# Leaving the context sums of an attention unnormalised, with beta as moving columns, split latent keys and wide softmax steps

## The chip, the cores and the metric

One core of a Trainium2 chip runs the kernel. The metric is device time in microseconds; the kernel before takes 1115.04 us, the median of three runs (1113.75 to 1117.1).

## What is computed

x is 8 batches of 100 tokens with 512 features. Three residual steps follow each other, each on a layernorm of x: a gated linear recurrence, a cross attention and a routed feed-forward. The change touches the attention:

```python
xn = _layernorm(x, gamma_media, beta_media)      # x here: the context, 8 x 722 x 512
ln = _layernorm(latents, gamma_lat, beta_lat)    # latents: layernorm of x, 8 x 100 x 512
q = ln @ Wq + bq
kv = jnp.concatenate([xn, ln], axis=1) @ Wkv + bkv
k, v = jnp.split(kv, 2, axis=-1)                 # 8 heads of 128
sim = jnp.einsum('bhid,bhjd->bhij', q * DH ** (-0.5), k)
out = jnp.einsum('bhij,bhjd->bhid', jax.nn.softmax(sim, axis=-1), v)
return out_transposed @ Wo + bo
```

## The kernel before

Everything is in float32, but the large products run in a faster form: each operand is split in a high and a low part and `split_products` (L575) issues three matmuls, high by high, high by low and low by high. Most have 400 moving columns.

Keys and values are never formed. The **q projection** (`project` on PE, 100 to 190 us) makes q per head for four batches at a time (a "half") and multiplies it by Wk, which gives queries in the space of the context rows ("qt"). ACT and DVE take each product out of its bank into one of the `st` buffers (L2039 on DVE), and SyncE stores them to `scr_q`. The latents serve as keys as well: `latent_keys` on DVE (L2012, L2014) adds their two parts up and subtracts the media's beta into `lks`, of which there are two, SyncE stores them to `scr_keys`, later loads one batch (`lk`), and `keys_of_latents` splits it again.

The **attention loop** goes over 16 units u, two per batch b (g = 0, 1), a unit being 4 heads by 100 latents, 400 columns. The 822 rows are 7 chunks: 6 of 128 and one of 54. A step does the scores of unit u (80 matmuls; ACT copies each bank to `pa` with the rms scale of the rows, L1426) and then the context sums of unit u-1, in four column blocks dc (80 matmuls). In between are small products: `turn_maxima` (L1111) transposes the running maxima so that DVE can reduce them, `spread_maxima` (L1118) brings the shift back to all rows, `spread_sums` (L1123) adds the sums of weights over the rows by a matrix of ones. DVE takes maxima (L1862, L1870), finds the shift (L1880 to L1886, result `dg`), adds it (L1894), adds up the weights (L1902, L1906), forms the low part of the weights (L1914, L1679), takes the reciprocal of the sums (L1923, 128x400, `inv`) and multiplies each context block by it on the way out of the bank (L1933, `zf`); ACT then adds beta (L1449), since the rows carry gamma but no beta. ACT does the exponentials (L1435) and the high part of the weights (L1441). In between, DVE prepares the next batch: statistics of rows (L1661, L1668), whose means go to DRAM and come back along the free axis as `mrow` (L676, L681), centred rows (L1675), centred keys (L1823, L1832), queries and the low rows `xn_l`. The order on each engine is written out by hand; DVE, ACT and SyncE take their instructions in that order.

`zf` goes to `scr_z`. The **value products** come after the loop: for each of 2 halves and 8 heads a unit of z (128x1600, `zr`) is loaded, split (ACT `z_h` L1471, DVE `z_l` L1679), multiplied by Wv on PE (12 matmuls), and its result split again (ACT `ot_h` L1485, DVE `ot_l` L1955) for the product with Wo. A list of events, run through by PE, ACT and DVE alike, each doing its part, sets the order: V a value product and its split, U the split of a unit of z, Y the output product of 128 tokens. It begins

```python
tail = [("V", 0), ("C", 0), ("U", 4), ("V", 1), ("U", 5), ("V", 2), ("U", 6), ("V", 3), ("V", 4), ("U", 7),
        ("V", 5), ("U", 8), ("V", 6), ("U", 9), ("V", 7), ("U", 10),
```

## Time and profile before

| | |
|---|---|
| median of 3 runs | 1115.04 us (1113.75 to 1117.1) |
| profiled execution, its time | 1109.71 us |
| its span | 1108.0 us |
| busy: TensorE / VectorE / ScalarE / GpSimd | 1021.8 / 879.2 / 595.3 / 129.9 us |
| mean granted TensorE clock | 0.964 |
| DMA | 177.62 MB, mean 160 GB/s |

PE is TensorE's matmul side, DVE VectorE, ACT ScalarE, SP SyncE. A share of busy time is a mean over stages; what bounds a stage is read from its own waits. Times in a timeline count from the start of the span. A matmul's row gives its whole duration; those of one stream overlap, so their cost is the distance of two starts.

### The profile page before, as it was taken

Reading aid. Unit: us, or ns where it says so; the run is one execution under the profiler, and the core shown is the slowest. Engines: PE = TensorE matmul, PEld = TensorE weight load, DVE = VectorE, ACT = ScalarE, POOL = GpSimd, SP = SyncE. Lnnn points to the kernel's source line nnn. Section 1 sums busy time; section 2 is a strip of 40 time slices with the busy share of each in tenths; the row PEclk is TensorE's granted clock in tenths of the full one; section 3 lists DMA queues with packets and bytes.
Section 4 is the critical chain, followed back from the end, with each engine's and each line's share of the span. In section 5 each row is a group of like instructions: output and inputs, shape, how many; then the busy total and the mean of one; then the engine's idle time right before and its main releaser. Section 6 shows DMA issues by size and latency. Waiting matters only on the chain. (4 is left out here: it accounts for less than half of the span.)

```text
span 1108.0 us, 14839 instructions
## 1 busy us (share of the span) xinstructions
PE 1021.8 (92%) x5178; PEld 926.5 (84%) x5179; DVE 879.2 (79%) x1206; ACT 595.3 (54%) x790; POOL 129.9 (12%) x107
## 2 busy tenths in 40 slices
PE   8998989569999998998989989799998999999997
PEld 7978878569899898998989989688886888888886
DVE  6988644878989989899998986687576993965992
ACT  4525455424665536555365554457344783856881
POOL 3525400000000000000000000000012021211221
PEclk9999889779999999999999999989998999999999
DMA  9313969303151332513234110726935992984980
GB/s 283 104 66 117 278 184 299 97 30 121 44 187 62 107 121 68 177 58 126 91 111 150 44 49 12 270 109 235 308 121 144 331 371 79 343 288 147 363 295 21
DMA packets 105886, 177.62 MB, mean 160 GB/s; under 512 B 28049, under 2 KB 48017, under 8 KB 105827
## 3 DMA queue, kind: packets, MB, share of 16 engines
q1 hardware_dynamic: 104146, 172.30, 47.1%
q0 software_dynamic: 1680, 4.54, 1.2%
q8 instruction: 36, 0.59, 0.3%
q14 instruction: 24, 0.19, 0.0%
HBM read 142.19 MB, written 35.61 MB: 160 GB/s over the span
## 5 line engine op out<-in xcount | busy, mean ns | idle before, releaser
L579 PE MATMUL bank<-ph,xn_h 128*128 128x400 f32 x384 | 145.7, 380 | 25.1 <-issue 13.5
L1679 DVE TENSOR_TENSOR wsl<-stage,wsh 128x2048 fp32r<-128x2048 f32 x63 | 143.8, 2292 | 21.9 <-ACT wsh L1476 17.3
L580 PE MATMUL bank<-pl,xn_h 128*128 128x400 f32 x384 | 137.6, 358 | 0.0
L579 PE MATMUL bank<-qt_h,xt_h 128*128 128x400 f32 x384 | 137.4, 358 | 0.0
L581 PE MATMUL bank<-ph,xn_l 128*128 128x400 f32 x384 | 136.9, 357 | 0.0
L580 PE MATMUL bank<-qt_l,xt_h 128*128 128x400 f32 x384 | 132.8, 346 | 0.0
L581 PE MATMUL bank<-qt_h,xt_l 128*128 128x400 f32 x384 | 132.1, 344 | 0.0
L1476 ACT CAST wsh<-stage 128x2048 fp32r<-128x2048 f32 x63 | 120.5, 1920 | 11.5 <-PE bank L581 8.4
L1426 ACT ACTIVATE pa<-bank,rsr 128x400 f32<-128x400 f32 x96 | 56.9, 595 | 110.8 <-PE bank L581 107.3
L579 PEld LDWEIGHTS bank<-ph,xn_h 128*128 128x128 f32 x384 | 76.1, 198 | 33.0 <-issue 19.1
L1449 ACT ACTIVATE zf<-zf,gbm 128x400 f32<-128x400 f32 x64 | 39.8, 621 | 79.6 <-DVE zf L1933 79.6
L580 PEld LDWEIGHTS bank<-pl,xn_h 128*128 128x128 f32 x384 | 76.2, 198 | 2.6 <-issue 0.3
L581 PEld LDWEIGHTS bank<-ph,xn_l 128*128 128x128 f32 x384 | 76.1, 198 | 0.0
L579 PEld LDWEIGHTS bank<-qt_h,xt_h 128*128 128x128 f32 x384 | 72.7, 189 | 2.3
L580 PEld LDWEIGHTS bank<-qt_l,xt_h 128*128 128x128 f32 x384 | 72.6, 189 | 2.2
L581 PEld LDWEIGHTS bank<-qt_h,xt_l 128*128 128x128 f32 x384 | 72.5, 189 | 0.0
L579 PE MATMUL bank<-wsh,xg_h 128*128 128x512 f32 x160 | 64.3, 402 | 2.0 <-issue 2.0
L579 PE MATMUL bank<-wsh,ht_h 128*128 128x512 f32 x160 | 65.0, 406 | 0.0
L580 PE MATMUL bank<-wsl,xg_h 128*128 128x512 f32 x160 | 62.9, 393 | 0.0
L581 PE MATMUL bank<-wsh,xg_l 128*128 128x512 f32 x160 | 62.9, 393 | 0.0
L581 PE MATMUL bank<-wsh,ht_l 128*128 128x512 f32 x160 | 62.6, 391 | 0.0
L580 PE MATMUL bank<-wsl,ht_h 128*128 128x512 f32 x160 | 62.3, 390 | 0.0
(269 smaller groups left out, 2414.1 us busy)
## 6 DMA issues: line engine op xcount, KB each, us to landing
stage<-in_W SPq DMA_DIRECT2D x63, 1024.0 KB, 6.6
scr_q<-st SPq DMA_DIRECT2D x16, 800.0 KB, 6.5
qf<-scr_q SPq DMA_DIRECT2D x16, 800.0 KB, 5.2
scr_z<-zf SPq DMA_DIRECT2D x16, 800.0 KB, 3.5
zr<-scr_z SPq DMA_DIRECT2D x16, 800.0 KB, 6.0
rt<-in_ctxT SPq DMA_DIRECT2D x7, 1444.0 KB, 6.3
raw<-in_ctx SPq DMA_DIRECT2D x8, 768.0 KB, 4.9
raw<-in_ctx SPq DMA_DIRECT2D x8, 512.0 KB
```

What stands on the lines that cost most here:

```text
L579: pe.matmul(dest, lh, rh, start=start and k == 0, stop=False)
L580: pe.matmul(dest, lh, rl, start=False, stop=False)
L581: last = pe.matmul(dest, ll, rh, start=False, stop=stop and k == n - 1)
L1426: act.activation(pa[k][:, c, :], score_bank(u, c)[:, 0:GR], ACT.Identity, scale=rss[b % 2][:, c:c + 1]).then_inc(s_ev, 1)
L1449: act.activation(at, at, ACT.Identity, bias=gbm[:, 1, dc:dc + 1]).then_inc(s_zbeta, 1)
L1476: act.copy(wsh[q][:], (first_last if made_in_place else stage[q % 4])[:]).then_inc(s_wh, 1)
L1679: return dve.tensor_tensor(dst, src, high.bitcast(F32), ALU.subtract)
```

## The change

- **Context sums.** ACT copies each context block out of its bank unscaled (`context_out`, in place of `add_shift`); `weighted` on DVE is gone. `spread_sums` gives the sums with the latents on the partitions (four matmuls with one moving column), and the reciprocal is of 100x4. The inverses of a batch are stored to `scr_inverse` (`store_inverse`) and loaded as rows over all partitions (`load_inverse`, 128x400, three buffers `ivt`), one per value product. DVE multiplies the value product by its row (`normalised`), ACT's `ot_h` and DVE's `ot_l` (event "v") then read `ivt`.
- **Beta.** It isn't added to z any more; two extra moving columns hold it (high and low part), so that a value product gives beta times Wv as two columns, which DVE adds to bv (`cb`, first half only). In the first half of the q projection two columns do the same for the latents. POOL's `shift_latents` is gone.
- **Latent keys.** The tokens' two parts are stored as they are and loaded from there straight into the split keys; `latent_keys` and `keys_of_latents` are gone. The load waits for the scores of the batch before.
- **Wide steps.** Maxima in operations of 800, 800, 400 and 54x400, sums likewise, low and high weights as 1200, 1200 and 54x400. The rms scale moves from the weights to the rows (`rows_high`, `rows_low`: six pieces with a scale).
- **Order.** In the loop the maxima of unit u are turned after context block 0 and spread after block 1. `rows_stats` of batch b+2 moves to the end of the odd unit, the queries ahead of the shift of the even one; SyncE stores the means ahead of z. In the last unit `values_low(2)` moves ahead of the shift and `values_low(3)` behind.

```diff
+XB = 2
+ZB = 2
+NIV = 3
...
-    d_lt = dram("scr_keys", (B, P, ND, LK))
+    d_lt = dram("scr_keys", (2, P, ND, NTOK))
+    d_iv = dram("scr_inverse", (2, HEADS, HT))
...
-    tail = [("V", 0), ("C", 0), ("U", 4), ("V", 1), ("U", 5), ("V", 2), ("U", 6), ("V", 3), ("V", 4), ("U", 7),
-            ("V", 5), ("U", 8), ("V", 6), ("U", 9), ("V", 7), ("U", 10),
+    tail = [("V", 0), ("C", 0), ("U", 4), ("V", 1), ("v", 0), ("U", 5), ("V", 2), ("v", 1), ("U", 6), ("V", 3), ("v", 2),
+            ("V", 4), ("v", 3), ("U", 7), ("V", 5), ("v", 4), ("U", 8), ("V", 6), ("v", 5), ("U", 9), ("V", 7), ("v", 6),
+            ("U", 10), ("v", 7),
             ("Y", 0), ("A", 0), ("B", 0), ("Y", 1), ("A", 1), ("B", 1), ("T", 0), ("Y", 2), ("A", 2), ("L", 0),
-            ("B", 2), ("T", 1), ("V", 8), ("U", 11), ("L", 1), ("T", 2), ("V", 9), ("U", 12), ("V", 10), ("U", 13), ("L", 2),
-            ("V", 11), ("U", 14), ("V", 12), ("U", 15), ("V", 13), ("V", 14), ("V", 15),
+            ("B", 2), ("T", 1), ("V", 8), ("U", 11), ("v", 8), ("L", 1), ("T", 2), ("V", 9), ("U", 12), ("v", 9),
+            ("V", 10), ("U", 13), ("v", 10), ("L", 2), ("V", 11), ("U", 14), ("v", 11), ("V", 12), ("U", 15), ("v", 12),
+            ("V", 13), ("V", 14), ("v", 13), ("V", 15), ("v", 14), ("v", 15),
...
+                sp.dma_start(xt_h[:, :, MEDIA:KLOW + KLAST].bitcast(F32), d_lt[0][:, :, at:at + T]).then_inc(s_ltin, 16)
+                sp.dma_start(xt_h[:, :, KLOW + DUP:KLOW + DUP + KLAST].bitcast(F32), d_lt[1][:, :, at + LAT0:at + T]
+                             ).then_inc(s_ltin, 16)
+                sp.dma_start(xt_l[:, :, MEDIA:KLOW].bitcast(F32), d_lt[1][:, :, at:at + LAT0]).then_inc(s_ltin, 16)
...
+            def store_inverse(b):
+                sp.wait_ge(s_inv, 2 * b + 2)
+                if b:
+                    sp.wait_ge(s_ivd, 16 * b)
+                sp.dma_start(d_iv[b // HALF, :, b % HALF * T:(b % HALF + 1) * T].rearrange("h t -> t h"), iv[0:T, b, :],
+                             allow_slow_non_contiguous=True).then_inc(s_ivd, 16)
+            def load_inverse(k):
+                half, h = divmod(k, HEADS)
+                if k >= NIV:
+                    sp.wait_ge(s_otl, ot_done(k - NIV))
+                if half and not h:
+                    sp.wait_ge(s_ivd, 16 * B)
+                if k >= 2:
+                    sp.wait_ge(s_ivl[k % 2], 16 * (k // 2))
+                sp.dma_start(ivt[k % NIV][:], bc(d_iv[half, h], HT)).then_inc(s_ivl[k % 2], 16)
...
+                sp.wait_ge(s_s, KC * (2 * b + 2))
+                load_latent_keys(b + 1)
+                sp.wait_ge(s_ktl, keys_done(b + 1))
                 if b + 2 < B:
                     load_keys(b + 2)
-                    load_latent_keys(b + 2)
+                    store_mean(b + 2)
+                    sp.wait_ge(s_nr, (b + 1) * 2)
+                    load_mean(b + 2)
...
+                    wide, out_tokens = bank[u % 4][:, 0:extra + HT], bank[u % 4][:, extra:extra + HT]
+                    for c in range(ND):
+                        high, low = wq_h[:, c, h * P:(h + 1) * P], wq_l[:, c, h * P:(h + 1) * P]
+                        pe.matmul(wide, high, xa_h[:, c, tokens_and_shift], start=c == 0, stop=False)
+                        pe.matmul(out_tokens, high, xa_l[:, c, cols], start=False, stop=False)
+                        last = pe.matmul(wide, low, xa_h[:, c, tokens_and_shift], start=False, stop=c == ND - 1)
+                    last.then_inc(s_qp, 1)
...
                 pe.wait_ge(s_dg, u + 1)
-                pe.matmul(mbank[:, 0:GR], ones[:], sm[:], start=True, stop=True).then_inc(s_spread, 1)
+                for j in range(GH):
+                    last = pe.matmul(mbank[0:T, j:j + 1], sm[:, 0, j * T:(j + 1) * T], ones[:, 0:1], start=True, stop=True)
+                last.then_inc(s_spread, 1)
...
-                            pe.wait_ge(s_otl, ot_done(k - 4))
-                        split_products(
-                            pe, bank[k % 4][:, 0:HT].rearrange("p (b t) -> p b t", b=HALF),
-                            [((wv_h[:, c, h * P:(h + 1) * P], wv_l[:, c, h * P:(h + 1) * P]),
-                              (z_h[zh_of[k]][:, :, c, :], z_l[zr_of[k]][:, :, c, :])) for c in range(ND)], True, True
-                            ).then_inc(s_vp, 1)
+                            pe.wait_ge(s_on, k - 3)
+                        wide, narrow = bank[k % 4][:, 0:HT + ZB], bank[k % 4][:, 0:HT].rearrange("p (b t) -> p b t", b=HALF)
+                        for c in range(ND):
+                            high, low = wv_h[:, c, h * P:(h + 1) * P], wv_l[:, c, h * P:(h + 1) * P]
+                            pe.matmul(wide, high, z_h[zh_of[k]][:, c, :], start=c == 0, stop=False)
+                            pe.matmul(narrow, high, z_l[zr_of[k]][:, :, c, :], start=False, stop=False)
+                            last = pe.matmul(wide, low, z_h[zh_of[k]][:, c, :], start=False, stop=c == ND - 1)
+                        last.then_inc(s_vp, 1)
...
-                    if u == 1 and c == 0:
+                    if u == 1 and c == 1:
                         turn_maxima(0)
-                    elif u == 1 and c == 2:
+                    elif u == 1 and c == 3:
                         spread_maxima(0)
                     elif u > 1 and c == 3:
                         spread_sums(u - 1)
                 if u == 1:
-                    context(0, 0)
                     spread_sums(0)
-                    context(0, 1)
-                    turn_maxima(1)
-                    context(0, 2)
-                    spread_maxima(1)
-                    context(0, 3)
+                if u < NU - 1:
+                    context(u - 1, 0)
+                    turn_maxima(u)
+                    context(u - 1, 1)
+                    spread_maxima(u)
...
+            def weights_high(u, part):
+                k, cs = u % 2, slice(PARTS[part][0], PARTS[part][-1] + 1)
+                act.wait_ge(s_exp, NP * u + part + 1)
+                if MC not in PARTS[part]:
+                    act.copy(ph[k][:, cs, :], pa[k][:, cs, :]).then_inc(s_ph, 1)
                 else:
-                    act.copy(ph[k][0:DUP, c, :], pa[k][0:DUP, c, :])
-                    act.copy(ph[k][DUP:P, c, :], pa[k][0:DUP, c, :]).then_inc(s_ph, 1)
-            def add_shift(u, dc):
-                act.wait_ge(s_zn, ND * u + dc + 1)
-                at = zf[u % 2][:, :, dc, :]
-                act.activation(at, at, ACT.Identity, bias=gbm[:, 1, dc:dc + 1]).then_inc(s_zbeta, 1)
+                    act.copy(ph[k][0:KLAST, MC, :], pa[k][0:KLAST, MC, :])
+                    act.copy(ph[k][DUP:DUP + KLAST, MC, :], pa[k][0:KLAST, MC, :]).then_inc(s_ph, 1)
+            def context_out(u, dc):
+                b, g = divmod(u, 2)
+                n = ND * u + dc
+                act.wait_ge(s_zb, n + 1)
+                if dc == 0 and b:
+                    act.wait_ge(s_zd[g], 16 * b)
+                act.copy(zf[g][:, :, dc, :], zbank[n % 2][:, 0:GR].rearrange("p (h t) -> p h t", h=GH)).then_inc(s_zn, 1)
...
-                        act.wait_ge(s_vp, k + 1)
+                        act.wait_ge(s_on, k + 1)
                         h = k % HEADS
                         if k == HEADS:
                             act.wait_ge(s_yd, T_A)
-                        act.activation(ot_h[:, h, OVER:], bank[k % 4][:, 0:HT], ACT.Identity, bias=bv[:, h:h + 1]
+                        act.activation(ot_h[:, h, OVER:], ivt[k % NIV][:], ACT.Identity, bias=cb[:, h:h + 1]
...
+            def first_sum(u):
+                dve.wait_ge(s_exp, NP * u + part_of(3) + 1)
+                if u:
+                    dve.wait_ge(s_spread, 2 * u)
+                ch.add(dve.tensor_tensor(sm[:], pa[u % 2][:, 0:2, :], pa[u % 2][:, 2:4, :], ALU.add))
                 ch.join()
-                ch.add(dve.tensor_tensor(sm[0:n, :], sm[0:n, :], pa[k][0:n, c, :], ALU.add))
-                if c == MC:
-                    tally(s_sum)
-            def weights_low(u, c):
-                b, k = u // 2, u % 2
-                dve.wait_ge(s_ph, KC * u + c + 1)
-                if c < MC:
-                    dve.scalar_tensor_tensor(pl[k][:, c, :], pa[k][:, c, :], rss[b % 2][:, c:c + 1], ph[k][:, c, :].bitcast(F32),
-                                             ALU.mult, ALU.subtract).then_inc(s_p, 1)
-                else:
-                    low(pl[k][0:DUP, c, :], pa[k][0:DUP, c, :], ph[k][0:DUP, c, :]).then_inc(s_p, 1)
+            def second_sum(u):
+                ch.add(dve.tensor_tensor(sm[:], sm[:], pa[u % 2][:, 4:6, :], ALU.add))
+                ch.join()
+            def last_sum(u):
+                ch.add(dve.tensor_tensor(sm[:, 0, :], sm[:, 0, :], sm[:, 1, :], ALU.add))
+                ch.join()
+                dve.wait_ge(s_exp, NP * u + NP)
+                ch.add(dve.tensor_tensor(sm[0:KLAST, 0, :], sm[0:KLAST, 0, :], pa[u % 2][0:KLAST, MC, :], ALU.add))
+                ch.join()
+            def weights_low(u, part):
+                k, cs = u % 2, slice(PARTS[part][0], PARTS[part][-1] + 1)
+                dve.wait_ge(s_ph, NP * u + part + 1)
+                n = KLAST if MC in PARTS[part] else P
+                low(pl[k][0:n, cs, :], pa[k][0:n, cs, :], ph[k][0:n, cs, :]).then_inc(s_p, 1)
+            def weights(u):
+                first_sum(u)
+                weights_low(u, 0)
+                second_sum(u)
+                weights_low(u, 1)
+                last_sum(u)
+                weights_low(u, 2)
             def inverse(u):
+                b, g = divmod(u, 2)
                 dve.wait_ge(s_spread, 2 * u + 2)
-                if u:
-                    dve.wait_ge(s_zn, ND * u)
-                dve.reciprocal(inv[:], mbank[:, 0:GR]).then_inc(s_inv, 1)
-            def weighted(u, dc):
-                b, g = divmod(u, 2)
-                n = ND * u + dc
-                dve.wait_ge(s_zb, n + 1)
-                if dc == 0:
-                    dve.wait_ge(s_inv, u + 1)
-                    if b:
-                        dve.wait_ge(s_zd[g], 16 * b)
-                dve.tensor_tensor(zf[g][:, :, dc, :], zbank[n % 2][:, 0:GR].rearrange("p (h t) -> p h t", h=GH),
-                                  inv[:].rearrange("p (h t) -> p h t", h=GH), ALU.mult).then_inc(s_zn, 1)
+                dve.reciprocal(iv[0:T, b, g * GH:(g + 1) * GH], mbank[0:T, 0:GH]).then_inc(s_inv, 1)
+            def normalised(k):
+                half, h = divmod(k, HEADS)
+                dve.wait_ge(s_vp, k + 1)
+                at, to = bank[k % 4], ivt[k % NIV]
+                if not half:
+                    ch.add(dve.tensor_tensor(cb[:, h:h + 1], at[:, HT:HT + 1], bv[:, h:h + 1], ALU.add))
+                    ch.join()
+                    ch.add(dve.tensor_tensor(cb[:, h:h + 1], at[:, HT + 1:HT + 2], cb[:, h:h + 1], ALU.add))
+                dve.wait_ge(s_ivl[k % 2], 16 * (k // 2) + 16)
+                dve.tensor_tensor(to[:], at[:, 0:HT], to[:], ALU.mult).then_inc(s_on, 1)
```

How this moves instructions, at two places. **VectorE, an odd unit of the steady loop**, from the end of the shifts of the unit before to its own last maximum (`pa` scores and weights, `pl` low weights, `sm` sums, `mx` maxima). Before:

```order
L1902 TENSOR_TENSOR sm<-pa_95 128x400
L1906 TENSOR_TENSOR sm<-sm,pa_95 128x400 x4
L1906 TENSOR_TENSOR sm<-sm,pa_95 54x400
L1914 SCALAR_TENSOR_TENSOR pl_99<-pa_95,rsr,ph_96 128x400 x3
L1862 TENSOR_TENSOR mx<-pa_97 128x400
...
L1679 TENSOR_TENSOR pl_99<-pa_95,ph_96 64x400
L1679 TENSOR_TENSOR xn_l<-raw,xn_h 128x1536
...
L1923 RECIPROCAL inv<-bank 128x400
...
L1679 TENSOR_TENSOR xn_l<-raw,xn_l 64x512
...
L1823 TENSOR_TENSOR rt<-rt,mrow 128x1444
```

With the change:

```order
L1966 TENSOR_TENSOR sm<-pa_91 128x800
L1739 TENSOR_TENSOR pl_95<-pa_91,ph_92 128x1200
L1970 TENSOR_TENSOR sm<-sm,pa_91 128x800
...
L1974 TENSOR_TENSOR sm<-sm 128x400
L1977 TENSOR_TENSOR sm<-sm,pa_91 54x400
L1739 TENSOR_TENSOR pl_95<-pa_91,ph_92 54x400
L1913 SCALAR_TENSOR_TENSOR xn_l<-raw,rsr,xn_h 128x512 x3
L1923 TENSOR_TENSOR mx<-pa_93 128x800
L1997 RECIPROCAL iv<-bank 100x4
...
L1739 TENSOR_TENSOR xn_l<-raw,xn_l 64x512
```

The operations on weights come as wide ones in turn with the sums, the reciprocal is small, and `keys_centred` (rt, mrow) no longer stands in the odd unit.

**ScalarE and VectorE, the value products** 0 to 2 (waits in brackets: s_vp by PE, s_on by DVE's multiplication, s_oth by ACT's ot_h, s_zh by ACT's z_h). ScalarE before:

```order
L1485 ACTIVATE ot_h<-bank,bv 128x400 [waits s_vp]
L1471 CAST z_h_131<-zr_124 128x1600 [waits s_vp,s_zl5]
L1485 ACTIVATE ot_h<-bank,bv 128x400 [waits s_vp]
L1471 CAST z_h_132<-zr_123 128x1600 [waits s_vp,s_zl4]
```

VectorE before:

```order
L1955 SCALAR_TENSOR_TENSOR ot_l<-bank,bv,ot_h 128x400 [waits s_oth]
...
L1679 TENSOR_TENSOR z_l_130<-zr_124,z_h_131 128x1600 [waits s_zh]
L1955 SCALAR_TENSOR_TENSOR ot_l<-bank,bv,ot_h 128x400 [waits s_oth]
L1679 TENSOR_TENSOR z_l_129<-zr_123,z_h_132 128x1600 [waits s_zh]
```

ScalarE with the change:

```order
L1537 ACTIVATE ot_h<-ivt_134,cb 128x400 [waits s_on]
L1523 CAST z_h_130<-zr_123 128x4x4x100 [waits s_vp,s_zl5]
L1537 ACTIVATE ot_h<-ivt_135,cb 128x400 [waits s_on]
L1523 CAST z_h_131<-zr_122 128x4x4x100 [waits s_vp,s_zl4]
```

VectorE with the change:

```order
L2004 TENSOR_TENSOR cb<-bank,bv 128x1 [waits s_vp]
L2006 TENSOR_TENSOR cb<-bank,cb 128x1 [waits s_dve]
L2008 TENSOR_TENSOR ivt_134<-bank,ivt_134 128x400 [waits s_ivl0]
...
L1739 TENSOR_TENSOR z_l_129<-zr_123,z_h_130 128x1600 [waits s_zh]
...
L2008 TENSOR_TENSOR ivt_135<-bank,ivt_135 128x400 [waits s_ivl1]
L2032 SCALAR_TENSOR_TENSOR ot_l<-ivt_134,cb,ot_h 128x400 [waits s_oth]
L1739 TENSOR_TENSOR z_l_128<-zr_122,z_h_131 128x1600 [waits s_zh]
```

ScalarE's ot_h waited for PE alone and now waits for VectorE, which has the multiplication into `ivt` ahead of ot_l; z_l of unit j stands between the products.

## Rows read from the trace of the kernel before

**Rows 1.** The page, section 1: busy time, share of the span and instructions of each engine.

```profile
PE 1021.8 (92%) x5178; PEld 926.5 (84%) x5179; DVE 879.2 (79%) x1206; ACT 595.3 (54%) x790; POOL 129.9 (12%) x107
```

**Rows 2.** Busy time by stretch: q projection, start of the attention loop, steady loop.

```profile
100.00:190.00 90.00, 78.96 (x424) 74.74 (x423) 49.34 (x81) 43.72 (x82) 12.38 (x9) 0.92 0.83 251
190.00:260.00 70.00, 48.44 (x208) 45.88 (x207) 51.80 (x80) 30.28 (x46) 2.35 (x2) 0.78 0.31 100
300.00:500.00 200.00, 188.88 (x995) 180.21 (x994) 185.59 (x284) 109.55 (x164) 4.78 (x6) 0.98 0.34 108
```

**Rows 3.** What PE waited for: us in total, times, longest us.

```profile
PE bank L1111 <- DVEq L1654: 20.3, 12, 9.7
...
PE bank L579 <- DVE zf L1933: 8.7, 3, 3.8
PE bank L1118 <- DVE dg L1886: 8.7, 7, 7.2
```

**Rows 4.** Timeline of PE, q projection: start us, us, instruction [idle before <-releaser].

```profile
99.71 0.34 PE L580 MATMUL bank<-qa_l,wk_h 128*128 128x400 f32 x1
...
105.91 0.34 PE L581 MATMUL bank<-qa_h,wk_l 128*128 128x400 f32 x1
...
112.91 0.70 PE L579 MATMUL bank<-qa_h,wk_h 128*128 128x400 f32 x1 [5.57 <-DVE st L2039]
...
152.82 0.70 PE L579 MATMUL bank<-qa_h,wk_h 128*128 128x400 f32 x1 [4.09 <-DVE st L2039]
```

**Rows 5.** Timeline of DVE, q projection.

```profile
111.19 0.57 DVE L2012 TENSOR_TENSOR lks<-xa_h,xa_l 128x400 f32<-128x400 f32 x1 [3.88 <-DMA scr_keys<-lks]
...
147.19 0.58 DVE L2012 TENSOR_TENSOR lks<-xa_h,xa_l 128x400 f32<-128x400 f32 x1 [9.86 <-DMA scr_keys<-lks]
```

**Rows 6.** Timeline of PE, one batch of the steady loop and the next one's first row.

```profile
407.94 0.64 PE L1111 MATMUL bank<-ident,mx 128*100 128x128 f32 x4 [0.85 <-DVEq L1654]
...
412.48 0.94 PE L1118 MATMUL bank<-dg,ones 100*128 100x400 f32 x2 [0.23 <-DVE dg L1886]
...
439.51 0.42 PE L579 MATMUL bank<-ph,xn_h 128*128 128x400 f32 x1 [2.08 <-issue]
...
443.26 0.65 PE L1111 MATMUL bank<-ident,mx 128*100 128x128 f32 x4 [1.33 <-DVEq L1654]
...
475.49 0.64 PE L1111 MATMUL bank<-ident,mx 128*100 128x128 f32 x4 [0.85 <-DVEq L1654]
```

**Rows 7.** Groups by line: count | busy us, mean ns | idle before, releaser.

```profile
L1923 DVE RECIPROCAL inv<-bank 128x400 f32<-128x400 f32 x16 | 42.3, 2641 | 0.0
...
L1933 DVE TENSOR_TENSOR zf<-bank,inv 128x400 f32<-128x400 f32 x64 | 36.0, 563 | 20.2 <-PE bank L1141 20.0
...
L1123 PE MATMUL bank<-sm,ones 128*128 128x400 f32 x32 | 13.3, 498 | 0.0
```

**Rows 8.** Timeline of SyncE's queue, batch 1 of the loop.

```profile
342.95 0.37 SPq L676 DMA_DIRECT2D scr_rows<-mvr  x1
351.45 0.32 SPq L681 DMA_DIRECT2D mrow<-scr_rows  x1
```

**Rows 9.** DMA issues: queue, operation, count, KB each, median us to landing.

```profile
zr<-scr_z SPq DMA_DIRECT2D x16, 800.0 KB, 6.0
...
mrow<-scr_rows SPq DMA_DIRECT2D x7, 361.0 KB, 4.8
...
lk<-scr_keys SPq DMA_DIRECT2D x8, 220.0 KB, 6.4
```

**Rows 10.** Groups by line, those of the value products.

```profile
L1679 DVE TENSOR_TENSOR z_l<-zr,z_h 128x1600 fp32r<-128x1600 f32 x16 | 29.0, 1819 | 5.5 <-ACT z_h L1471 5.5
...
L1471 ACT CAST z_h<-zr 128x1600 fp32r<-128x1600 f32 x16 | 24.3, 1526 | 4.2 <-DMA zr<-scr_z 4.2
...
L1955 DVE SCALAR_TENSOR_TENSOR ot_l<-bank,bv,ot_h 128x400 fp32r<-128x400 f32 x16 | 10.0, 630 | 5.4 <-ACT ot_h L1485 5.1
...
L1485 ACT ACTIVATE ot_h<-bank,bv 128x400 fp32r<-128x400 f32 x16 | 9.4, 594 | 8.4 <-PE bank L581 8.3
```

488 lines of the change are left out of this document (223 added, 265 removed).

## Prediction

> **What bounds the kernel now.** I read the page first, then the busy time by stretch, then the waits of PE, then timelines at the places that these name. TensorE is busy for 1021.8 of 1108.0 us [rows 1], so a gain must come out of the 86 us in which PE idles, out of what it loses at the lower clock, or out of its own work. The stretches [rows 2] say where: the q projection (100 to 190) idles 11.0 us, the start of the attention loop (190 to 260) 21.6 us at a granted clock of 0.78, the steady loop only 11.1 us in 200. The waits of PE [rows 3] say for whom: VectorE, for maxima, shifts and the context blocks it takes away; in the steady loop it is busy for 185.6 of 200 us. An "issue" wait is one that the view can't name; the one at 439.51 [rows 6] is of a context product that waits for the low part of the rows, the last thing DVE had written.
>
> **q projection.** Matmuls start every 0.182 us at the full clock (34 starts from 99.71 to 105.91 [rows 4]); 424 of them need 77.2 us, and the stretch takes 90, so 12.8 us are waits and slow matmuls. The two long waits, 5.57 and 4.09 us, are for a DVE copy of a bank [rows 4]. Why was it late? DVE stood at the latent keys, whose two buffers wait for their own transfers: 3.88 us before 111.19, 9.86 before 147.19 [rows 5]. The change deletes these steps; the keys go to DRAM from the split tokens, which no engine waits for. New here: two more columns in 8 groups of 8 matmuls (64 x 2 columns, 2/400 of 0.182 us each: under 0.1 us), two one-column ACT operations for each of 8 heads (between nothing, where ACT idles, and 16 x 0.6 us by the 400-column ot_h row [rows 10]; ACT waits for PE there, so I take nothing), and more bytes out (3.3 MB for 1.9 MB, in the stretch where the q stores also run). What is late next is the ring of q stores. I leave 0.8 us of it: **-12** (-9 to -13).
>
> **Start of the loop.** 208 matmuls are busy for 48.4 us; at the steady loop's 0.190 us each (188.88/995) they would be 39.5. With the idle 21.6 that is 30.5 us lost. What makes it: DVE does the row statistics and maxima of unit 0, the 400-wide sums and low weights, a 2.64 us reciprocal [rows 7] and the multiplications of the context, all one after the other, while PE has nothing yet to cover it; the longest wait is 9.7 us for the first maxima [rows 3]. The change puts the low rows ahead, turns the maxima one score chunk later, halves the number of DVE operations and takes the reciprocal from 400 columns to 4. I walk through it with the durations of the rows: first maxima about 3.3 us of wait, sums before the first context 5.4, second maxima 2.0, together 10.7, and about 5 at the low clock behind them. 30.5 - 15.7: **-15** (-10 to -19).
>
> **Steady loop, units 2 to 14.** A batch of two units takes 67.55 us (407.94 to 475.49), of which PE waits 0.85 + 0.23 + 2.08 + 1.33 = 4.5 [rows 6]; other batches wait somewhat less. By the 11.1 us idle in 200 [rows 2] it is 24 us from 272 to 707, and the clock of 0.98 there, against 1.00 undisturbed, stands for two short stretches at half speed, 3 us more: 27 in all. What a DVE operation costs beside its columns comes from two rows: 1.819 us for 1600 columns [rows 10], 0.563 for 400 [rows 7], so 1.05 ns a column and 0.14 us for each operation. VectorE sheds, per unit, the wide reciprocal but for some 0.15 (2.5 us), four products of 0.56 (2.25), and 0.14 for each of nine operations fewer in maxima, sums and low weights, with their handovers (1.4): some 6 us. Per batch it sheds the splitting of the latent keys too (1 us) and gains as much by low rows in six pieces with a scale. It was busy for 185.6/200 x 67.55 = 62.7 us of a batch and will be for about 51, and the waits for maxima and low rows should go. ScalarE takes the four copies out of the bank in place of four additions of the shift: the same count, but now released by PE and not by DVE. Against it stand two things. The sums are now spread by four small matmuls (with 100 columns as weights and one moving column, four passes each) for one of 400 columns, 2 x 0.50 us [rows 7]; between the same time and 0.8 us, taken at +0.12 per unit, 2 us in all. And the row mean: DVE now takes the statistics of batch b+2 after the shift of the odd unit, so the store of the means goes out later; the store and load take 8.5 us (342.95 to 351.45 [rows 8]) and 4.8 us [rows 9], and DVE, in order, wants the mean about 4 us before it lands. Most of that is DVE's slack; I let 1 us per batch through to PE, 6 in all. 27 - 2 - 6: **-19** (-11 to -26).
>
> **Last unit** (707 to 751). The 7.2 us wait for dg [rows 3] was DVE in front of value weights whose load had been issued too late; it still is, but a third of them now comes behind the first. **-1** (-3 to +3).
>
> **Value products (the tail).** This is what the change costs. Before, ScalarE wrote ot_h straight from PE's bank and could run ahead of DVE; a step was bound by PE, 12 x 0.182 = 2.2 us, or by DVE's z_l + ot_l, 1.73 + 0.54 = 2.3. Now DVE must first multiply the bank by the inverse row, ot_h waits for that, and both queues go in the order V(k), U(j), V(k+1). So the engines take turns: ACT ot_h 0.49 and z_h 1.53, DVE z_l 1.76, two one-column additions (0.14 each by the reckoning above, 0.35 with the handover between them; no row shows one, and two 400-column ones would be 1.1) and the multiplication 0.57: 4.7 us. In the second half ot_l stands in the chain, 0.54 in place of the 0.35: 4.9. The durations are those of [rows 10], less up to 0.1 where the engine's next row begins before this one ends; the multiplication has that of zf in [rows 7], the same shape and source. PE and the beta columns (2/400 again) are hidden under it. First half: 7 steps with a U, 7 x 2.4 = 17, less the 4.2 us that ACT used to wait for z units [rows 10] (the last z goes out of ACT's copy, without DVE's queue ahead) and 1.3 at the start: +11.5. Second half: 5 steps x 2.6 = 13, less 3 for the last products, which need no unit: +10. Between them PE idles and comes back at the low clock: +2. **+23.5** (+10 to +32).
>
> **Sum.** -12 - 15 - 19 - 1 + 23.5 = -23.5 against the profiled execution's 1109.7, so 1086; the median of the three runs is 5.3 us above it, which gives **1091**, as 1091.5 rounded down.
>
> **A page against the rows.** The trace shows the 220 KB load of the latent keys land in 6.4 us [rows 9], in runs of 1760 bytes. The change loads twice the bytes in runs of 400, 216 and 184. They may start when PE has done the scores of a batch and must be there one context later, 80 matmuls or about 15 us; with twice 6.4 us they are in time, and the sum has nothing for them.
> The Trainium skill, "DMA: Bandwidth & Descriptors", Specifications, asks for at least 512 bytes for line rate. By that rule the change goes the wrong way, and it would make the case below of late keys.
> No row here has runs of that size, so the trace neither bears it out nor denies it.
>
> **Rivals.**
> *The softmax keeps its waits (0.17).* DVE's saved time buys nothing, since the mean row lands late and each batch waits for it as long as it waited for DVE. For it: the store of 3 KB that takes 8.5 us [rows 8] now starts about 16 us into a unit. Against it: DVE's slack of 12 us per batch. Half the steady gain and 5 of the start's go: 1091 + 10 + 5 = 1106.
> *The tail is mild (0.15).* If DVE had its multiplications done while ACT is at z_h, a step would be bound by DVE's own sum, 1.73 + 0.54 + 0.57 + 0.35 = 3.2, and not 4.7: 12 steps x 1.6 = 19 less, 1072. Against it: the queues are in order, and the excerpt of VectorE's order puts z_l of the next unit ahead of the next product.
> *The keys are late (0.05).* 320 to 400 KB in 1536 short runs land after more than 15 us; each microsecond beyond costs PE one in each of 7 batches. At 19 us: +28, and 1119.
> *Slower: the inverse rows are late (0.10).* Each product needs its row of inverses, a 205 KB load into one of three buffers, issued when the product three before is done, in one queue with 800 KB units that take 6.0 us [rows 9]. The step of 4.8 us gives it three steps, 14.4 us, of which the engines' own part takes about 4: it decides from 10 us to landing on. The gain of 23.5 is gone when 12 steps cost 2 us more each, at 16 us to landing. At 18 us the steps take 7.5 us: 12 x 2.7 = +32, and 1123. Against it: a load of 361 KB of the same kind lands in 4.8 us [rows 9].
> That the change doesn't remove what it says it does I rule out for the latent keys and the reciprocal: neither stands in DVE's new order.
>
> **Chances.** My forecast 0.53, the others as above. The range: 1066 to 1110 holds the forecast over most of what its terms' bounds allow, the mild tail and the kept waits, and leaves out the two slow cases and some of each edge. A measurement here can tell 0.3%, 3.3 us, from no change. Faster: 0.53 + 0.15 + most of 0.17, so 0.82; same 0.05; slower 0.13.
>
> **What would show it.** Right: no DVE wait on scr_keys, q stretch with under 3 us of PE idle; PE waits for L1111 down from 20.3 to about 6; PE idle in 200 us of the loop under 5 us; in the tail ACT's ot_h released by DVE, 4.7 to 4.9 us from one ot_h to the next, and PE below 50% busy for some 60 us. Wrong: ot_h every 3.2 us or less; ot_h or DVE's multiplication released by a DMA; PE released by a DMA into xt_h at the start of a batch; PE waits for keys or shifts of over 2 us per batch.

## The result and the profile after

The changed kernel takes 1084.24 us (median of 4, 1084.0 to 1084.45) against 1114.39 us (4 runs) before: a ratio of 0.9725, 95% interval 0.9708 to 0.9743. Forecast were 1091 (1066 to 1110). The profiled execution of after takes 1084.0 us and is 25.7 us shorter than that of before, which lay 4.7 below its median; the stages below are compared on these two.

Read from the timelines of PE, where each stage's first matmul starts (us):

| stage begins with | before | after | stage's length, before to after |
|---|---|---|---|
| q projection | 79.1 | 83.4 | stage ahead of it: +4.3 |
| first scores | 175.4 | 165.8 | q projection 96.3 to 82.4: -13.9 |
| scores of unit 2 | 254.3 | 225.6 | start of the loop 78.9 to 59.8: -19.1 |
| scores of unit 15 | 690.2 | 639.9 | units 2 to 14, 435.9 to 414.3: -21.6 |
| value product 0 | 751.3 | 697.7 | last unit 61.1 to 57.9: -3.2 |
| feed-forward | 840.1 | 813.5 | value products and routing 88.8 to 115.7: +26.9 |
| end of PE | 1101.3 | 1075.6 | feed-forward 261.2 to 262.1: +0.9 |

The page of after, busy time, answers to [rows 1]:

```profile
PE 1011.3 (93%) x5274; PEld 925.5 (86%) x5275; DVE 795.0 (73%) x1052; ACT 580.2 (54%) x770; POOL 119.4 (11%) x100
```

VectorE lost 84 us of work, from 879.2 to 795.0. TensorE lost 10 us of busy time though it has 96 instructions more; its mean granted clock is 0.975 in place of 0.964, so fewer matmuls ran at the lower level. Busy time by the same stretches as [rows 2]:

```profile
100.00:190.00 90.00, 85.59 (x480) 81.72 (x479) 51.12 (x90) 52.10 (x101) 10.11 (x7) 0.99 0.78 254
190.00:260.00 70.00, 62.13 (x328) 60.12 (x328) 60.93 (x80) 33.35 (x46) 2.34 (x2) 0.94 0.36 100
300.00:500.00 200.00, 195.64 (x1097) 192.16 (x1096) 163.40 (x226) 106.23 (x155) 6.98 (x6) 1.00 0.41 121
```

PE idles 4.4 us in 200 of the steady loop, and VectorE has 37 us to spare there. What PE waits for now (us, times, longest; compare [rows 3]):

```profile
PE bank L1211 <- DVE z_l L1739: 14.3, 7, 3.2
PE bank L1165 <- DVE dg L1952: 8.5, 3, 7.4
PE bank L587 <- DMA xt_l<-scr_keys: 7.3, 5, 1.7
PE bank L587 <- DVE ot_l L2032: 7.0, 2, 3.7
PE bank L1171 <- DVE pl L1739: 5.9, 1, 5.9
PE bank L1158 <- DVEq L1714: 4.1, 2, 2.9
```

The waits for maxima fell from 20.3 to 4.1 us. In their place stand waits for z_l and ot_l, which belong to the value products, and one for latent keys, which is new. Groups by line, for [rows 7] and [rows 10]:

```profile
L1498 ACT COPY zf<-bank 128x400 f32<-128x400 f32 x64 | 31.6, 494 | 101.7 <-PE bank L1190 101.4
...
L1739 DVE TENSOR_TENSOR z_l<-zr,z_h 128x1600 fp32r<-128x1600 f32 x16 | 29.0, 1822 | 22.4 <-ACT z_h L1523 22.4
...
L1523 ACT CAST z_h<-zr 128x1600 fp32r<-128x1600 f32 x16 | 24.3, 1520 | 0.0
...
L2032 DVE SCALAR_TENSOR_TENSOR ot_l<-ivt,cb,ot_h 128x400 fp32r<-128x400 f32 x16 | 10.0, 628 | 0.4 <-ACT ot_h L1537 0.4
L1537 ACT ACTIVATE ot_h<-ivt,cb 128x400 fp32r<-128x400 f32 x16 | 10.0, 628 | 41.7 <-DVE ivt L2008 41.7
...
L1997 DVE RECIPROCAL iv<-bank 100x4 f32<-100x4 f32 x16 | 2.8, 176 | 4.0 <-PE bank L1171 3.9
```

The reciprocal went from 2641 to 176 ns. ot_h now waits 41.7 us in all for VectorE's multiplication (L2008), and z_l 22.4 us for ScalarE's z_h. One step of the value products, on ScalarE:

```profile
707.61 0.63 ACT L1537 ACTIVATE ot_h<-ivt,cb 128x400 fp32r<-128x400 f32 x1 [2.63 <-DVE ivt L2008]
708.15 1.51 ACT L1523 CAST z_h<-zr 128x1600 fp32r<-128x1600 f32 x1
712.30 0.63 ACT L1537 ACTIVATE ot_h<-ivt,cb 128x400 fp32r<-128x400 f32 x1 [2.63 <-DVE ivt L2008]
```

and on VectorE:

```profile
705.01 1.83 DVE L1739 TENSOR_TENSOR z_l<-zr,z_h 128x1600 fp32r<-128x1600 f32 x1 [2.05 <-ACT z_h L1523]
706.75 0.15 DVE L2004 TENSOR_TENSOR cb<-bank,bv 128x1 f32<-128x1 f32 x1
706.94 0.16 DVE L2006 TENSOR_TENSOR cb<-bank,cb 128x1 f32<-128x1 f32 x1
707.01 0.56 DVE L2008 TENSOR_TENSOR ivt<-bank,ivt 128x400 f32<-128x400 f32 x1
707.49 0.63 DVE L2032 SCALAR_TENSOR_TENSOR ot_l<-ivt,cb,ot_h 128x400 fp32r<-128x400 f32 x1
709.69 1.83 DVE L1739 TENSOR_TENSOR z_l<-zr,z_h 128x1600 fp32r<-128x1600 f32 x1 [1.57 <-ACT z_h L1523]
```

The two engines take turns: z_l at 705.01, the two additions and the multiplication to 707.57, ot_h at 707.61, z_h to 709.66, the next z_l at 709.69. A step is 4.68 us, of which ScalarE waits 2.63 us for VectorE and VectorE 1.6 to 2.1 us for ScalarE.

Two things were not foreseen. Ahead of the first scan VectorE has three tiny operations, on 4 and 8 columns:

```profile
34.10 1.25 DVE L1795 CAST bmx<-gbm 128x4 fp32r<-128x4 f32 x1
35.38 1.21 DVE L1739 TENSOR_TENSOR bmx<-gbm,bmx 128x4 fp32r<-128x4 f32 x1
36.62 1.22 DVE L1799 CAST xa_h<-bmx 128x8 fp32r<-128x8 f32 x1
```

They take 1.2 us each. GpSimd is busy with its additions at that time:

```profile
28.23 13.24 POOL L930 TENSOR_TENSOR xin<-xin,boa 100x512 f32<-100x512 f32 x8
```

They don't make the whole +4.3, though: VectorE's operation in front of them already starts at 30.81 us in this execution and at 28.96 in that of before.

And batches 2 to 6, five of the eight, begin with a wait of PE for the keys of the latents; two of these waits:

```profile
291.88 0.42 PE L587 MATMUL bank<-qt_h,xt_h 128*128 128x400 f32 x1 [1.73 <-DMA xt_l<-scr_keys]
```

```profile
355.37 0.42 PE L587 MATMUL bank<-qt_h,xt_h 128*128 128x400 f32 x1 [1.32 <-DMA xt_l<-scr_keys]
```

### The profile page after: what moved, and what is told of

It reads as the page before. It is cut to its first block, busy times and chain, and to the rows that moved or that the text cites. A ratio compares the mean times of both kernels' runs of the same rounds, so it can differ in the third digit from the quotient of the medians.

```text
span 1082.3 us, 14817 instructions
## 1 busy us (share of the span) xinstructions
PE 1011.3 (93%) x5274; PEld 925.5 (86%) x5275; DVE 795.0 (73%) x1052; ACT 580.2 (54%) x770; POOL 119.4 (11%) x100
## 4 chain that ended last, share of the span: by engine, by line
PE 60%; DVE 15%; DMA 10%; ACT 6%; SPq 5%; issue 4%; POOL 0%; DVEq 0%; POOLq 0%; ACTq 0%
PE bank L587 17%; PE bank L588 16%; PE bank L589 16%; DMA xt_l<-scr_keys 4%; ACT xn_h L1457 2%; DVE z_l L1739 2%; DMA scr_rows<-mvr 2%; ACT z_h L1523 2%; PE bank L1334 2%; DVE str__65 L1721 1%; SPq L694 1%; PE bank L1072 1%; DMA w<-in_WoT 1%; PE bank L1074 1%; PE bank L1073 1%
## 5 line engine op out<-in xcount | busy, mean ns | idle before, releaser
L587 PE MATMUL bank<-ph,xn_h 128*128 128x400 f32 x384 | 140.2, 365 | 1.6 <-DVE pl L1739 1.6
L587 PE MATMUL bank<-qt_h,xt_h 128*128 128x400 f32 x384 | 134.8, 351 | 7.3 <-DMA xt_l<-scr_keys 7.3
L588 PE MATMUL bank<-pl,xn_h 128*128 128x400 f32 x384 | 133.3, 347 | 0.0
L589 PE MATMUL bank<-ph,xn_l 128*128 128x400 f32 x384 | 132.5, 345 | 0.0
L1498 ACT COPY zf<-bank 128x400 f32<-128x400 f32 x64 | 31.6, 494 | 101.7 <-PE bank L1190 101.4
L587 PEld LDWEIGHTS bank<-ph,xn_h 128*128 128x128 f32 x384 | 73.1, 190 | 4.6 <-issue 1.8
L588 PEld LDWEIGHTS bank<-pl,xn_h 128*128 128x128 f32 x384 | 73.1, 190 | 2.4 <-issue 0.3
L589 PEld LDWEIGHTS bank<-ph,xn_l 128*128 128x128 f32 x384 | 73.0, 190 | 0.0
L1739 DVE TENSOR_TENSOR pl<-pa,ph 128x1200 fp32r<-128x1200 f32 (+1 forms) x48 | 54.1, 1128 | 23.0 <-ACT ph L1487 22.1
L1960 DVE TENSOR_TENSOR pa<-pa,bank 128x1200 f32<-128x1200 f32 (+1 forms) x48 | 51.1, 1119 | 17.3 <-PE bank L1165 17.3
```

What stands on the lines that cost most here:

```text
L587: pe.matmul(dest, lh, rh, start=start and k == 0, stop=False)
L588: pe.matmul(dest, lh, rl, start=False, stop=False)
L589: last = pe.matmul(dest, ll, rh, start=False, stop=stop and k == n - 1)
L1498: act.copy(zf[g][:, :, dc, :], zbank[n % 2][:, 0:GR].rearrange("p (h t) -> p h t", h=GH)).then_inc(s_zn, 1)
L1739: return dve.tensor_tensor(dst, src, high.bitcast(F32), ALU.subtract)
L1960: dve.tensor_tensor(at, at, nbank[0:n, 0:GR].unsqueeze(1).broadcast_to([n, len(cs), GR]), ALU.add).then_inc(s_sub, 1)
```

## The experiments

All were compared with the kernel before on the same chip. Where the text speaks of a stage, it is measured on the profiled execution as in the table. The change itself was not run again beside the experiments, and the kernel before had medians of 1111.9 to 1113.9 us there against 1114.39 beside the change. So a difference of two medians against the change is 1 to 3 us uncertain, and for small gains the ratio to before says more: the change has 0.9725.

**ScalarE's units ahead of its products.** In ScalarE's list of events each U stands ahead of the V that it followed; VectorE's and PE's lists stay.

```diff
+    act_tail = list(tail)
+    for i in range(len(act_tail) - 1):
+        if act_tail[i][0] == "V":
+            n = i + 1
+            while act_tail[n][0] in "Cv":
+                n += 1
+            if act_tail[n][0] == "U":
+                act_tail.insert(i, act_tail.pop(n))
...
-            finish(tail)
+            finish(act_tail)
```

> The changed kernel with one order edited: ScalarE splits the next unit of z before it writes ot_h, and not after. Theory (the two engines take turns, 4.68 us a step in the trace of the change): ScalarE's copy of the next unit then runs beside VectorE's work, a step falls to VectorE's own sum, 1.75 + 0.30 + 0.50 + 0.50 + small waits, 3.2 to 3.4 us, 12 steps save about 1.4 each: 17 us, about 1067 (1062 to 1072). Rival A (the rows of inverses set the pace): each is loaded only when the ot_l three before is done and lands 4.4 us later, so VectorE's multiplication waits for the DMA and a step stays over 4.2 us: 1078 or more. Rival B (value products wait for units of z from DRAM): ScalarE's copies wait for the DMA, same size as rival A.

1069.23 us (ratio 0.9621, 0.9598 to 0.9645): 15 less by the medians, 11.6 by the ratios. From value product 0 to the feed-forward it takes 102.7 us in place of 115.7, 13.0 less. The turns are gone, but the DMA becomes the next bound; ScalarE and then VectorE:

```profile
702.48 1.54 ACT L1531 CAST z_h<-zr 128x1600 fp32r<-128x1600 f32 x1 [0.90 <-DMA zr<-scr_z]
...
706.46 1.53 ACT L1531 CAST z_h<-zr 128x1600 fp32r<-128x1600 f32 x1 [1.91 <-DMA zr<-scr_z]
...
714.93 1.53 ACT L1531 CAST z_h<-zr 128x1600 fp32r<-128x1600 f32 x1 [0.81 <-DMA zr<-scr_z]
```

```profile
712.88 0.57 DVE L2016 TENSOR_TENSOR ivt<-bank,ivt 128x400 f32<-128x400 f32 x1 [1.49 <-DMA ivt<-scr_inverse]
```

z_h waits 0.8 to 4.5 us for its unit, the multiplication 0.3 to 1.5 us for its row of inverses. From one ot_h to the next it is 2.7 to 4.0 us in the first half and 3.0 to 6.6 in the second, so theory and rivals A and B each hold a part: the hand-over was what bound, and behind it lie the loads.

**The normalisation left out.** PE, ScalarE and VectorE as before the change in this stage, no inverse rows.

```diff
-                            pe.wait_ge(s_on, k - 3)
+                            pe.wait_ge(s_otl, ot_done(k - 4))
-                        act.wait_ge(s_on, k + 1)
+                        act.wait_ge(s_vp, k + 1)
-                        act.activation(ot_h[:, h, OVER:], ivt[k % NIV][:], ACT.Identity, bias=cb[:, h:h + 1]
+                        act.activation(ot_h[:, h, OVER:], bank[k % 4][:, 0:HT], ACT.Identity, bias=bv[:, h:h + 1]
-                        normalised(k)
```

> The changed kernel with the normalisation of the value products left out: no load of inverse rows, no multiplication and no sum of beta on VectorE; ot_h and ot_l read the bank and ot_h waits for PE alone, as before the change. The output is unnormalised. Theory (the whole 27 us that the stage of value products grew by comes from this hand-over): first to last value product takes 61 to 64 us again in place of 88, the kernel 1058 to 1062. Rival (part of the growth has another cause, such as the wider and strided z parts or the end of the loop having less to cover the start of the stage): the stage takes 70 us or more, the kernel 1067 or more.

The whole kernel (1097.75 us) is no measure here: with unnormalised values the tokens are routed otherwise, and the feed-forward has 1152 matmuls with the experts' weights in place of 960 and takes 309.3 us instead of 262.1. To its start: 781.2 us against 813.5. From value product 0 to the feed-forward it takes 85.8 us; after had 115.7, before 88.8. All of the growth, and 3 us more, is the normalisation.

**Unnormalised sums alone, in the kernel before.** ScalarE copies each block from the bank with beta as its bias; VectorE's products are gone, its reciprocal is of 4 columns.

```diff
-                act.wait_ge(s_zn, ND * u + dc + 1)
-                act.activation(at, at, ACT.Identity, bias=gbm[:, 1, dc:dc + 1]).then_inc(s_zbeta, 1)
+                act.wait_ge(s_zb, n + 1)
+                act.activation(zf[g][:, :, dc, :], zbank[n % 2][:, 0:GR].rearrange("p (h t) -> p h t", h=GH), ACT.Identity,
+                               bias=gbm[:, 1, dc:dc + 1]).then_inc(s_zbeta, 1)
-                dve.reciprocal(inv[:], mbank[:, 0:GR]).then_inc(s_inv, 1)
+                dve.reciprocal(inv[:, 0:GH], mbank[:, 0:GH]).then_inc(s_inv, 1)
```

> The kernel before with part one of the change alone, in the loop only: VectorE's multiplications of the context blocks gone and its reciprocal of 4 columns instead of 400, ScalarE copies each block from the bank and adds beta in the same operation. Maxima, sums, weights, latent keys, the order and the value products are as before. The output is unnormalised. Theory (VectorE's work per unit is what PE waits for in the loop, and the 4.8 us per unit are the larger part of it): unit 2 to the end of the loop shortens by 14 to 20 us and the start of the loop by 5 to 8, together 1114.4 to about 1092 (1088 to 1097). Rival (the waits come from the place of the maxima and the low rows in the order, not from the amount of work): the waits for maxima stay, and the gain is 8 us or less: 1106 or more.

Here too the feed-forward is longer (309.3 us) and the total, 1119.43, says nothing. Up to the feed-forward it is 38.1 us shorter than before, more than the theory had. Units 2 to 14 take 410.1 us, a pair of them 63.1: less than in the full change (414.3). The stretch 300 to 500 us:

```profile
300.00:500.00 200.00, 198.21 (x1067) 190.81 (x1066) 174.11 (x274) 115.84 (x174) 4.79 (x6) 1.00 0.38 119
```

1.8 us idle in 200. The last unit gains 6.8, the value products 3.4, the start of the loop only 3.1 us. The edit also takes VectorE out from between the bank and ScalarE; in the steady loop that is not what PE waited for, as none of its three waits for zf [rows 3] lies between 254 and 690 us.

**Narrow steps.** The changed kernel, its wide operations cut to 400 columns.

```diff
-                ch.add(dve.tensor_tensor(sm[:], pa[u % 2][:, 0:2, :], pa[u % 2][:, 2:4, :], ALU.add))
+                for j in range(2):
+                    ch.add(dve.tensor_tensor(sm[:, j, :], pa[u % 2][:, j, :], pa[u % 2][:, 2 + j, :], ALU.add))
...
-                low(pl[k][0:n, cs, :], pa[k][0:n, cs, :], ph[k][0:n, cs, :]).then_inc(s_p, 1)
+                for c in range(cs.start, cs.stop):
+                    last = low(pl[k][0:n, c, :], pa[k][0:n, c, :], ph[k][0:n, c, :])
+                last.then_inc(s_p, 1)
```

> The changed kernel with the wide softmax operations cut back: maxima, sums, low weights and high weights in operations of 400 columns, in the same places of the order and with the same releases. Theory (the wide steps are not what shortened the loop: the kernel before with unnormalised sums alone already has a batch of 63.2 us in the loop): some 12 operations more per unit at 0.08 to 0.14 us each, 1.2 us of 32, lie in the slack of VectorE and ScalarE; a batch stays at 63.6 us, the kernel within 3 us of the changed one, 1084 to 1087, the few us from the start of the loop, where PE waits for the sums. Rival (VectorE is still close to the bound): a batch grows by 1 us or more and the kernel to 1091 or more.

1084.52 us against the change's 1084.24 (ratios 0.9745 and 0.9725, with intervals that overlap). Units 2 to 14 take 414.8 us (414.3), the start of the loop 61.7 (59.8, and 57.8 to 59.5 in the other runs that leave it as it is). The wide steps are worth 2 to 4 us at the start and nothing in the loop.

**Beta's small operations later.**

```diff
             dve.wait_ge(s_ca, 16 * N_CA)
-            ch.add(dve.tensor_copy(bmx[:, :, 0], gbm[:, 1, :]))
...
             low_states(ND - 1)
             low_weight(6)
+            ch.add(dve.tensor_copy(bmx[:, :, 0], gbm[:, 1, :]))
...
```

> The changed kernel with three small VectorE operations (beta split in two parts and copied beside the tokens, 4 and 8 columns) moved from ahead of the first scan to behind the last. In the trace of the change they take 1.25, 1.21 and 1.22 us each at 34.1 to 37.8, while GpSimd runs its additions. Theory (they stand at the head of VectorE's chain of scans, which PE waits for, and cost the 4.3 us by which the q projection starts later): it starts 3 to 4 us earlier, the kernel about 1080.5. Rival A (GpSimd's extra subtraction of beta, 1.3 us ahead of the additions, or the later first loads are the cause): less than 1.5 us. Rival B (the time is lost again at the first scores, which wait for a store or a load): the q projection starts earlier and the loop doesn't.

1079.89 us (ratio 0.9705, 2.2 us less by the ratios). The q projection starts at 79.2, 4.2 us earlier. The same three operations, with GpSimd idle:

```profile
61.52 0.16 DVE L1823 CAST bmx<-gbm 128x4 fp32r<-128x4 f32 x1
61.71 0.17 DVE L1739 TENSOR_TENSOR bmx<-gbm,bmx 128x4 fp32r<-128x4 f32 x1
61.91 0.17 DVE L1827 CAST xa_h<-bmx 128x8 fp32r<-128x8 f32 x1
```

0.16 to 0.17 us each. But the edit doesn't own all of the 4.2. The operation in front (the low part of a weight) starts at 28.97 us here, at 28.96 in the kernel before and at 30.81 in the change's profiled execution; in the others it starts between 28.8 and 30.7, whatever the edit, so most of these 1.9 us is variation. Behind it, the first of the operations on gates (`og`, L1813 in the change, 800 columns) takes 1.66 us both here and in the kernel before and 0.56 in the change: it pays there the delay beside GpSimd that the small operations have paid in the change. From the end of the weight's operation to the end of `og` it is 4.1 us in the change and 1.6 here: the three operations cost some 2.5 us. The starts of the q projection agree, 81.0 to 83.4 in the six kernels with these operations in front and 79.1 to 81.1 in the six of before's kind.

**Latent keys first in SyncE's queue.**

```diff
-                    load_rows_raw(b + 2)
-                sp.wait_ge(s_qtl, 2 * (b + 1) + 1)
-                load_queries(b + 1, 1)
                 sp.wait_ge(s_s, KC * (2 * b + 2))
                 load_latent_keys(b + 1)
+                    load_rows_raw(b + 2)
+                sp.wait_ge(s_qtl, 2 * (b + 1) + 1)
+                load_queries(b + 1, 1)
```

> The changed kernel with one order edited on SyncE: the three loads of a batch's latent keys are issued ahead of the loads of the next context rows and queries, not behind them. Theory (PE waits 1.3 to 1.7 us at the start of batches 2 to 6 for these keys, because six other issues stand ahead and the three themselves take 7.4 us to issue; batch 7, with no rows to load, doesn't wait): the waits go, 7 us less, about 1077.5. Rival A (the short runs are slow whatever stands ahead of them): they land as late after the issue and PE still waits over 0.8 us per batch. Rival B (the rows come later by as much and make VectorE's statistics and the mean row late): the gain is under 3 us and a wait on statistics or the mean row appears.

1078.11 us, 6 less by the medians, 2.9 by the ratios (0.9699 and 0.9725); no wait for the keys is left. Units 2 to 14 take 411.0 us, for 412.9 to 414.8 where the order is as in the change, so the loop keeps 2 to 4 of the 7.3 us. Part of it comes back as waits for the shift (L1165), 11.6 us in all against 8.5, one of them:

```profile
437.75 0.60 PE L1165 MATMUL bank<-dg,ones 100*128 100x400 f32 x1 [1.39 <-DVE dg L1952]
```

In five batches VectorE now waits 2.3 to 3.5 us for the row mean, where it waits 0.8 to 2.4 in the change: that is rival B's wait, and the gain of 2 to 4 us in the loop lies about at its bound of 3.

The place in the queue was the cause, not the length of the runs. In the change the three loads are issued 3.7 us behind the first load of the rows, and take 7.4 us to issue:

```profile
337.66 0.40 SPq L643 DMA_DIRECT2D raw<-in_ctx  x1
...
341.33 0.61 SPq L693 DMA_DIRECT2D xt_h<-scr_keys  x1
341.98 2.92 SPq L694 DMA_DIRECT2D xt_h<-scr_keys  x1
344.95 3.88 SPq L696 DMA_DIRECT2D xt_l<-scr_keys  x1
```

The same three loads of the same batch in this run:

```profile
334.17 0.52 SPq L693 DMA_DIRECT2D xt_h<-scr_keys  x1
334.74 0.63 SPq L694 DMA_DIRECT2D xt_h<-scr_keys  x1
335.41 1.64 SPq L696 DMA_DIRECT2D xt_l<-scr_keys  x1
```

From the first issue to the last landing it is 4.8 us here and 13.8 in the change, with runs of the same length. In the change too the last batch, which has no rows loaded in front, issues its three in 1.9 us, and they land in 4.6 to 4.9 us each where the others take 7.2 to 10.2.

**Value weights behind the softmax weights in the last unit.**

```diff
                     for k in range(3):
                         keys_transposed(b + 1, k)
-                elif g:
-                    values_low(0)
-                    values_low(1)
...
-                elif g:
-                    values_low(2)
...
             weights(NU - 1)
-            values_low(3)
+            for k in range(ND):
+                values_low(k)
```

> The changed kernel with the low parts of the value weights moved, in the last unit, from ahead of the shift to behind the softmax weights. In both traces PE waits over 7 us there for the shift, which stands in VectorE's queue behind value weights that have only just been loaded. Theory (that order is the cause): the wait of 7.4 us goes, the products that follow have their weights in time, 5 to 8 us less, about 1078. Rival (the weights are then late for the first value product, as all of VectorE's work for the tail comes behind): the wait moves to the start of the value products and the gain is under 3 us.

1076.99 us, 7 less by the medians, 4.1 by the ratios (0.9688 and 0.9725), of which 3.8 in the last unit. The wait of 7.4 us goes, and one of 3.8 us for ScalarE's copy of a context block comes: the rival's kind of shift, to another engine.

**The q projection: keys written straight from the tokens, in the kernel before.**

```diff
-                sp.wait_ge(s_lkd, b + 1)
-                sp.dma_start(d_lt[b][:, :, 0:T], lks[b % 2][:]).then_inc(s_ltout[b % 2], 16)
+                sp.wait_ge(s_tel, b + 1)
+                x = xa_h[:, :, b * T:(b + 1) * T].bitcast(F32)
+                sp.dma_start(d_lt[b][:, :, 0:T], x).then_inc(s_ltout[b % 2], 16)
```

> The kernel before without VectorE's part in the latent keys: scr_keys is written straight from the high part of the tokens, in the same sizes and at the same places of the queue; low part and the subtraction of beta are left out. Theory (VectorE stood at these steps, and PE's two long waits came from that): the q projection shortens by 10 to 13 us, 1114.4 to about 1103. Rival (the transfers themselves are the bound, the stores of q wait behind them whoever writes the keys): the bank copies wait for the store ring instead, 5 us or less: 1109 or more.

1103.08 us, 10 less (ratio 0.9921, 0.9897 to 0.9944), which is the theory's number; but the profiled executions differ by 6.2 us, the stage itself goes from 96.3 to 90.7 us only, and what PE waits for is the rival's. ScalarE:

```profile
110.75 1.29 ACT L1525 ACTIVATE st<-bank 128x400 f32<-128x400 f32 x3 [3.13 <-DMA scr_q<-st]
...
114.90 1.30 ACT L1525 ACTIVATE st<-bank 128x400 f32<-128x400 f32 x3 [2.46 <-DMA scr_q<-st]
...
119.07 1.30 ACT L1525 ACTIVATE st<-bank 128x400 f32<-128x400 f32 x3 [2.49 <-DMA scr_q<-st]
...
123.61 1.30 ACT L1525 ACTIVATE st<-bank 128x400 f32<-128x400 f32 x3 [2.86 <-DMA scr_q<-st]
...
157.09 0.90 ACT L1525 ACTIVATE st<-bank 128x400 f32<-128x400 f32 x2 [3.57 <-DMA scr_q<-st]
```

The wait for VectorE's keys became one for the ring of q stores. Two further runs ask what holds that ring.

**Their stores together, ahead of the q stores.**

```diff
             write_residuals(range(HALF))
+            for b in range(HALF):
+                write_latent_keys(b)
...
-                    if not half and h < HALF:
-                        write_latent_keys(h)
```

> The kernel before without VectorE's part in the latent keys, as in the run before it, and with the stores of the first four batches' keys issued together ahead of the stores of q, not one between every two of these. Left out: the low part and beta in these keys. In the run before it, the waits for VectorE had turned into waits of ScalarE and VectorE for the ring of q stores (2.5 to 3.6 us each), and the stage took 90.7 us where the change takes 82.4. Theory (the eight stores of keys between the q stores, 1.2 to 1.9 us of issue for each pair, hold the ring back): the stage takes 83 to 86 us. Rival (the first q store is late anyway, at 103 to 105 us, since four stores of latents stand ahead of it that wait for GpSimd's subtraction of beta): 89 us or more, as the key stores now also stand ahead of it.

The stage takes 95.7 us, with one wait of 12.2 us; 1109.64 us over 10 runs with a wide spread (1104.81 to 1114.77). The rival.

**And without GpSimd's subtraction.** As above, and

```diff
-                    sp.wait_ge(s_lnw, b + 1)
+                    sp.wait_ge(s_lnr, b + 1)
...
-            shift_latents(range(B))
```

> The kernel of the run with keys early, and GpSimd's subtraction of beta from the latents left out, so that SyncE stores them as soon as VectorE has written them. Left out: that subtraction, and low part and beta in the keys. Theory (the subtraction paces the queue in front of the q stores, 1.8 us for each batch): the first q store goes out before 100 us instead of 103 to 105, no wait for the ring is over 1 us, and the stage takes 82 to 84 us, what the change reaches. Rival (bandwidth: 12.8 MB of q and 3 to 5 MB of others in 90 us): the waits for the ring stay and the stage takes 86 us or more.

1094.04 us (ratio 0.9820, 0.9805 to 0.9835); the stage takes 83.5 us, 12.2 less than in the run before it and within a microsecond or so of the change. By the medians it is 19.8 us less than before, by the profiled executions 12.3, which is this stage; what the medians have beyond that is open. GpSimd's subtractions and SyncE's queue in the kernel before:

```profile
91.08 8.79 POOL L902 TENSOR_TENSOR xh<-xh,bm 100x512 f32<-100x512 f32 x4 [0.18 <-POOL rsa L860]
```

```profile
92.84 7.33 SPq L664 DMA_DIRECT2D scr_latents<-xh  x4
...
103.12 0.72 SPq L700 DMA_DIRECT2D scr_q<-st  x1
```

and here:

```profile
72.46 3.71 SPq L664 DMA_DIRECT2D scr_latents<-xh  x4
...
100.77 2.55 SPq L703 DMA_DIRECT2D scr_q<-st  x2
```

The stores of latents, which waited for GpSimd in front of the q stores, are out 20 us earlier, and the queue then stands idle until the first q store. So of the 13.9 us of this stage VectorE's keys, taken out first, explain under half (5.6 us); the larger part comes when GpSimd's pace in SyncE's queue goes too. The subtraction alone, with VectorE's keys left in, was not taken out, so how much each is worth by itself is open.

**Maxima first, in the kernel before.**

```diff
-            rows_stats(1, 0)
             maximum(0, 1)
-            rows_stats(1, 1)
...
                         shift(0, part)
+                    rows_stats(1, 0)
+                    rows_stats(1, 1)
+                    rows_norm(1, 0)
+                    rows_norm(1, 1)
```

> The kernel before with one order edited on VectorE: at the start of the loop the statistics and centring of the second batch's rows come behind the shift of unit 0, not between its maxima. In the trace of before VectorE waits there 5.3 and 5.1 us for the load of these rows with the maxima behind them. Theory (this order, and not the width or number of operations, made most of what the start of the loop lost): from the first scores to those of unit 2 it takes 8 to 12 us less than the 78.9, the kernel about 1103. Rival A (the work itself bounds it, so that the statistics only wait elsewhere): less than 4 us. Rival B (the row means are now late for the keys of batch 1): the gain comes back as a wait of VectorE for the mean row and of PE for the keys at unit 2.

1109.13 us, 4.7 less (ratio 0.9954, 0.9939 to 0.9970); the start of the loop takes 75.0 us for 78.9, and as the runs that leave it alone have 76.7 to 78.9, the order is worth 2 to 4 us. The wait for the first maxima is gone, and PE waits at the next place instead:

```profile
217.89 0.67 PE L579 MATMUL bank<-ph,xn_h 128*128 128x400 f32 x1 [10.22 <-DVE pl L1914]
```

Rival A: VectorE's work as a whole has to be done there, in whatever order.

**All four edits.** ScalarE ahead, beta later, keys first, value weights behind.

> The changed kernel with all four edits that shortened it one by one: ScalarE's units of z ahead, beta's small operations behind the scans, latent keys first in SyncE's queue, low value weights behind the softmax weights in the last unit. Theory (they are in different stages and add up, 15 + 4 + 6 + 7 less what one takes from another): 1084.2 to about 1053 (1050 to 1058). Rival (they overlap: with the tail no longer taking turns its DMA loads set the pace, and an earlier end of the loop finds the units of z not loaded): 1060 or more.

1067.69 us (ratio 0.9597, 0.9579 to 0.9616), the fastest median here, but only 1.5 us below ScalarE's order alone, whose interval (0.9598 to 0.9645) overlaps: the rival, though not quite as it said. The q projection starts 4 us earlier, and the value products take 104.6 us, 2 more than with ScalarE's order alone. Units 2 to 14 take 414.9 us, no less than without the edits: PE waits for maxima and shifts at nearly every batch's first unit (0.3 to 1.95 us). And the last unit gains little: ScalarE stands at the value weights' load with its copy of the context behind it, first ScalarE's row, then PE's.

```profile
660.69 1.99 ACT L1510 CAST wv_h<-wv 128x1024 fp32r<-128x1024 f32 x2 [9.02 <-DMA wv<-in_Wv]
```

```profile
665.14 0.70 PE L595 MATMUL bank<-ph,xn_h 128*128 128x400 f32 x1 [5.50 <-ACT zf L1506]
```

Which of the edits spoils which in the loop wasn't tried. The row mean is a candidate: VectorE waits 2.6 to 3.7 us a batch for it here, as in the run with the keys first.

## Why the prediction was right, and where not

- **Sum.** -23.5 was forecast against the profiled execution and -25.7 measured there. That is 2 of the 7 us by which 1091 missed 1084.24. The rest is mostly the 5.3 us that the forecast added because the profiled execution of before lay so far below its median; the four runs of the change lie within 0.5 us of each other, and its profiled one is 0.2 below the median. Two terms that weren't in it, +4.3 ahead of the q projection and +0.9 behind, are hidden in that by gains larger than said.
- **q projection**, -12 (-9 to -13): -13.9, just outside. The size was near, the reason half right. "The keys go to DRAM from the split tokens, which no engine waits for" holds, but the step "POOL's `shift_latents` is gone" was priced at nothing, and it carries the larger part when it is taken out last, 12.2 us. So that the size came near was in part luck.
- **Start of the loop**, -15 (-10 to -19): -19.1, 0.1 outside. The waits came as walked through (2.9 for 3.3, 5.9 for 5.4, none of 2.0). Of the gain, unnormalised sums alone give 3.1, the order of the statistics 3.9 and the wide steps 1.9, each to 2 us or so; they add up to 9 of the 19.1, and what the parts do together was not separated.
- **Steady loop**, -19: -21.6. The mechanism, VectorE's work per unit, is shown: unnormalised sums alone give it all (-25.8), with a batch of 63.1 us. VectorE is busy for 52 us of a batch (163.40/200 x 63.7), for the 51 forecast. The term of +6 for the late mean row did not show: VectorE does wait up to 2.4 us for it, but PE's waits for the shift in units 2 to 14 come to 1.1 us. The 7.3 us of waits for keys stood in its place, and partly in front of it: with these gone, PE waits for the shift in six of these units, 0.2 to 1.4 us each, 4.9 in all. That the row mean is behind this is argued from VectorE's waits for it, not shown by a run.
- **Keys**: the rival had 0.05 and a threshold of 15 us. It came in a small form, with one of the signs that the forecast named for being wrong, PE released by a load into xt_l at the start of a batch. What the forecast missed is the queue: the three loads stand behind 1.75 MB of rows and 0.8 MB of queries and take 7.4 us to issue. By the Trainium skill, "DMA: Bandwidth & Descriptors", Specifications, runs under 512 bytes miss line rate. In the change, 92 KB in runs of 184 bytes do land in 9.7 us where 220 KB in runs of 1760 took 6.4 [rows 9]. But issued first, in the steady loop, they land in 3.4 to 3.9 us, so the rule would have named the wrong cause for most of it.
- **Last unit**, -1 (-3 to +3): -3.2 by the table, which begins it with the scores of unit 15. The forecast begins it with the context products behind them, at 707; from there it is 44.3 us before and 42.6 after, -1.7, inside the range, and the loop then has -23.2.
- **Value products**, +23.5: +26.9, and the runs put all of it on the normalisation. The step was forecast at 4.7 us and is 4.68. The terms that helped were too large: 4.2 us of waits for units and 1.3 at the start were to be won back. In the second half steps are 5.0 to 5.7 us, not 4.9. One sign that the forecast named did not come: PE was to be below 50% busy for some 60 us, and in the seven steps of the first half (697.7 to 733) it is busy for 25.4 of 35.3 us.
- **Late inverse rows**: nothing of it in the change, since the turns leave 14 us; with ScalarE ahead they cost 0.3 to 1.5 us in some steps, as a bound behind the bound.
- **What was left out.** "Cost at nothing" for small operations needs a look at what else runs. Three of them were not in the sum at all; they stood at the head of the chain of scans with GpSimd busy, at 1.2 us for what takes 0.16, and made some 2.5 of the +4.3 us.

## What to carry over

When a normalisation is moved behind a product, look at the engine that turns round between two others there: two queues that go V, U, V, U on both sides take turns, and letting one of them run a step ahead was worth 13 us in its stage, where the whole change brought 30. Follow a queue back to its slowest writer: the q stores waited for GpSimd through stores that had nothing to do with them. And edits that each gain in their own stage are to be run together before they are added up.

## What was not expected of the hardware

VectorE's operations on 4 to 8 columns took 1.21 to 1.25 us while GpSimd ran an addition over 100x512 and 0.16 to 0.17 us without. By the Trainium skill, "SBUF — State Buffer", SBUF: two separate sides, GpSimd and VectorE take turns at one pair of memory ports, held for a whole instruction, when VectorE has two inputs from SBUF or copies in a mode that uses both ports; the rows agree, with 1.1 us of delay where one of GpSimd's additions takes 1.65 (13.24/8). The delay went by the operation and not by its size: `og` with its 800 columns lost the same 1.1 us (1.66 for 0.56) in the kernel before, where it stood in that place.

How long a load holds SyncE's queue when it is issued depended on what stood in front of it. The loads of 108 and 92 KB, in runs of 216 and 184 bytes, took 2.9 and 3.9 us to issue behind 2.5 MB of others (batch 3) and landed in 8.6 and 10.2 us; in the run with the keys first, with the same runs and no rows in front, they took 0.6 and 0.6 to 1.6 us to issue and landed in 3.1 to 3.9.
